# Count blocks that end on a real product instead of a product with zeros, and half-size loop turns where two chunks are left

## What is computed

```
def _sage_layer(h, edge_src, edge_dst, deg_inv, W_self, W_neigh, b):
    msg = h[edge_src]
    agg = jax.ops.segment_sum(msg, edge_dst, num_segments=h.shape[0])
    mean = agg * deg_inv[:, None]
    return h @ W_self + mean @ W_neigh + b
...
deg = jax.ops.segment_sum(jnp.ones_like(edge_dst, dtype=x.dtype), edge_dst, num_segments=N)
deg_inv = 1.0 / jnp.maximum(deg, 1.0)
h = jax.nn.relu(_sage_layer(x, edge_src, edge_dst, deg_inv, W_self0, W_neigh0, b0))
out = _sage_layer(h, edge_src, edge_dst, deg_inv, W_self1, W_neigh1, b1)
...
x = x + _L0_gnn_ref(_layernorm(x, axis=-1), src, dst, ...)
x = x + _L0_ffn_ref(_layernorm(x, axis=-1)[None], L0_ffn_W_fc, L0_ffn_W_proj)[0]
```

## Time and profile before

| | |
|---|---|
| median of the runs | 1630.81 us |
| profiled execution | 1631.58 us |
| its span in the trace | 1629.6 us |
| TensorE busy with products | 1603.5 us |
| stretch with count turns | 60 to 303 us |
| granted TensorE clock, mean | 0.996 |

### The profile page before, as it was taken

How to read it: one execution, slowest core, us unless ns; L and a number is a source line. 1 busy time by engine, 2 the same in 40 slices (tenths; PEclk the granted TensorE clock), 3 DMA queues, 4 the chain that set the end, 5 groups by cost and what they waited for, 6 DMA issues and landing times.

```text
span 1629.6 us, 22403 instructions
## 1 busy us (share of the span) xinstructions
PE 1603.5 (98%) x7709; PEld 1344.4 (83%) x7709; DVE 894.4 (55%) x1613; ACT 462.8 (28%) x816; POOL 97.9 (6%) x190
## 2 busy tenths in 40 slices
PE   7999999999999999999999999999999999999997
PEld 5777667788888888889899899898998888888884
DVE  7786777565212222656334343343443788888868
ACT  3344454211112000114123131130321333333358
POOL 0230134200000000001000000000001000000000
PEclk9999999999999999999999999999999999999998
DMA  7322333467533454558122021120223233333321
GB/s 296 133 104 82 115 114 130 178 246 261 186 103 121 186 206 159 180 194 287 50 78 78 26 103 51 51 103 26 77 69 111 104 116 116 116 116 116 116 91 49
DMA packets 55926, 205.43 MB, mean 126 GB/s; under 512 B 5330, under 2 KB 13852, under 8 KB 50340
## 3 DMA queue, kind: packets, MB, share of 16 engines
q1 hardware_dynamic: 53524, 191.76, 33.3%
q0 software_dynamic: 2320, 12.58, 2.0%
HBM read 153.85 MB, written 50.47 MB: 125 GB/s over the span
## 4 chain that ended last, share of the span: by engine, by line
PE 95%; issue 1%; DVE 1%; DMA 1%; ACT 1%; DVEq 0%; POOL 0%; SPq 0%; ACTq 0%; POOLq 0%
PE bank L1588 26%; PE bank L1569 26%; PE bank L1425 26%; PE bank L1518 11%; PE bank L1374 3%; PE bank L1401 2%; ACT spikes L900 1%; PE bank L1620 0%; DMA w_landing<-w_self 0%; DVE w L1079 0%; DMA pr_raw<-w_proj 0%; DMA at_dram<-counts_tile 0%; DMA rows<-x 0%; DVE key_hot L1026 0%; DVE xt L1067 0%
## 5 line engine op out<-in xcount | busy, mean ns | idle before, releaser
L1425 PE MATMUL bank<-w,xt 128*128 128x512 f32 x1920 | 462.7, 396 | 2.6 <-DVE w L1079 2.6
L1569 PE MATMUL bank<-x2t,fc_w 128*128 128x384 f32 (+1 forms) x2304 | 438.4, 350 | 0.4 <-ACT relu L865 0.4
L1569 PEld LDWEIGHTS bank<-x2t,fc_w 128*128 128x128 f32 x2304 | 411.7, 188 | 25.6 <-issue 0.7
L1425 PEld LDWEIGHTS bank<-w,xt 128*128 128x128 f32 x1920 | 356.8, 189 | 76.9 <-issue 3.3
L1588 PE MATMUL bank<-pr_w,hid 128*128 128x512 f32 (+1 forms) x1824 | 418.7, 390 | 0.0
L1588 PEld LDWEIGHTS bank<-pr_w,hid 128*128 128x128 f32 (+1 forms) x1824 | 338.2, 185 | 75.5
L1291 DVE TENSOR_TENSOR y<-y,bank 128x512 f32<-128x512 f32 (+1 forms) x152 | 104.2, 687 | 214.8 <-PE bank L1588 214.8
L1518 PE MATMUL bank<-z,at 128*128 128x512 f32 x800 | 186.9, 392 | 0.0
L1518 PEld LDWEIGHTS bank<-z,at 128*128 128x128 f32 x800 | 148.8, 188 | 30.2
L860 ACT ACTIVATE pr_w<-pr_raw 128x1024 fp32r<-128x1024 f32 x64 | 67.1, 1049 | 365.6 <-PE bank L1588 362.6
L1234 DVE TENSOR_TENSOR square<-relu 128x384 f32<-128x384 f32 (+1 forms) x96 | 56.9, 592 | 144.2 <-ACT relu L865 144.2
(11 more groups left out here) (127 smaller groups left out, 931.8 us busy)
## 6 DMA issues: line engine op xcount, KB each, us to landing
fc_raw<-w_fc SPq DMA_DIRECT2D x64, 512.0 KB, 4.3
pr_raw<-w_proj SPq DMA_DIRECT2D x64, 512.0 KB, 3.5
xt<-xt_dram SPq DMA_DIRECT2D x24, 1024.0 KB, 5.0
xt_dram<-xt SPq DMA_DIRECT2D x18, 1024.0 KB, 4.3
at<-at_dram SPq DMA_DIRECT2D x20, 640.0 KB, 5.9
part_dram<-rows SPq DMA_DIRECT2D x20, 512.0 KB, 3.8
rows<-part_dram SPq DMA_DIRECT2D x20, 512.0 KB, 4.5
rows<-x SPq DMA_DIRECT2D x18, 512.0 KB, 4.9
```

Source lines behind the costliest of these rows:

```text
L1425: ins = nc.tensor.matmul(bank[:, 2 * (u % 2) + q, :], xt[j][:, a, k, :], w[:, k, b, q * HALF:(q + 1) * HALF], start=(k == 0 and m == 0), s ...
L1569: ins = nc.tensor.matmul(bank[:, 4 + (c if g == 0 else j % 2), 0:n], fc_w[:, j % 2, k, a, :], x2t[g][:, k, v, c0:c0 + n], start=(k == 0 an ...
```

## The change

It has four parts. A window without extra turns now multiplies two of its head chunks, runs its loop, and ends on the third head chunk, which carries `stop` and counts up `hot_used[HEAD_SET]`. A window with extra turns runs the loop to its true end first, in turn 0, and then the turns that run once; the last of them carries `stop`. The product with `zero_w` is gone, and so are `zero_w` and `counts_summed`: ScalarE waits for `hot_used` of the set that ends the block. In 17 windows (`SHORT_TURNS`) the loop of turn 0 covers two chunks a turn instead of four, one in set 1 and one in set 2. And the turns are spread anew: unit 0 of S0 gets 2 turns for 3, unit 4 gets 6 for 7, units 6 and 7 get 7 for 6. There are still 74 turns. On TensorE and VectorE the registers are read and added up after the head, no longer before it.

```diff
+SHORT_TURNS = {0, 6, 9, 10, 11, 12, 13, 18, 27, 31} | set(range(33, 40))
+
+def chunks_of_set(i, j):
+    return 1 if j == 0 and window_of(i) in SHORT_TURNS else LOOP_SET
...
-        [(A0 + 3, 1, 30, 12)] + [(A0 + n, 3, 14, 36) for n in range(4, TILES - 1)] + [(A0 + 9, 1, 12, 12), (S0, 3, 30, 18)]
-        + [(S0 + p, 6 if p in (6, 7) else 7, 0, 48) for p in range(1, 9)]):
+        [(A0 + 3, 1, 30, 12)] + [(A0 + n, 3, 14, 36) for n in range(4, TILES - 1)] + [(A0 + 9, 1, 12, 12), (S0, 2, 40, 10)]
+        + [(S0 + p, 6 if p == 4 else 7, 0, 48) for p in range(1, 9)]):
...
             first, end = registers[2 * (i % 2):2 * (i % 2) + 2]
-            if j > 0:
-                engine.reg_add(first, first, LOOP_CHUNKS)
-            if j < extra_turns(i):
-                engine.reg_add(stop, first, 1)
-                end = stop
-            latest = CHUNKS + HEAD_CHUNKS - 1 + LOOP_CHUNKS * j
+            latest = CHUNKS + HEAD_CHUNKS - 1
+            if j == 0:
+                latest += LOOP_CHUNKS * extra_turns(i)
+                engine.reg_add(edge, first, LOOP_CHUNKS * extra_turns(i))
+                first = edge
+            else:
+                latest += LOOP_CHUNKS * (j - 1)
+                if j > 1:
+                    engine.reg_add(first, first, LOOP_CHUNKS)
+                engine.reg_add(edge, first, 1)
+                end = edge
...
-                with act.Fori(first, end, LOOP_CHUNKS) as g:
+                with act.Fori(first, end, count * len(LOOP_SETS)) as g:
...
-                act.wait_ge(counts_summed, i + 1)
+                if extra_turns(i) > 0:
+                    act.wait_ge(hot_used[ACT_SET], visit)
+                else:
+                    act.wait_ge(hot_used[HEAD_SET], i + 2)
...
             def key_one_hots(i, j):
                 v = window_of(i)
-                first, end = turns_of_step(dve, registers, stop, i, j)
                 if j == 0:
                     dve.wait_ge(current_ready, i + 1)
...
                     ins.then_inc(key_hot_ready[HEAD_SET], 1)
-                with dve.Fori(first, end, LOOP_CHUNKS) as g:
+                count = chunks_of_set(i, j)
+                first, end = turns_of_step(dve, registers, edge, i, j)
+                with dve.Fori(first, end, count * len(LOOP_SETS)) as g:
...
             def step_of_edges(i, j):
-                first, end = turns_of_step(pe, registers, stop, i, j)
+                last = extra_turns(i)
                 if j == 0:
                     if i >= 2:
                         pe.wait_ge(counts_copied, i - 1)
-                    products_of_set(i, HEAD_SET, i + 1, start=True)
-                with pe.Fori(first, end, LOOP_CHUNKS) as g:
-                    for s in LOOP_SETS:
-                        products_of_set(i, s, visit)
-                    pe.reg_add(visit, visit, 1)
-                    pe.reg_add(next_visit, next_visit, 1)
-                if j == extra_turns(i):
-                    nc.tensor.matmul(bank[:, 4 + i % 2, 0:2], zero_w[:, :], iota[0:P, 0:2], start=False,
-                                     stop=True).then_inc(counts_summed, 1)
+                    pe.wait_ge(src_hot_ready, i + 1)
+                    pe.wait_ge(key_hot_ready[HEAD_SET], i + 1)
+                    kept = 0 if last else 1
+                    for c in range(HEAD_CHUNKS - kept):
+                        ins = product_of_chunk(i, HEAD_SET, c, start=(c == 0))
+                    if not kept:
+                        ins.then_inc(hot_used[HEAD_SET], 1)
+                count = chunks_of_set(i, j)
+                first, end = turns_of_step(pe, registers, edge, i, j)
+                with pe.Fori(first, end, count * len(LOOP_SETS)):
+                    turn_of_edges(i, count, stop=(j == last > 0))
+                if last == 0:
+                    product_of_chunk(i, HEAD_SET, HEAD_CHUNKS - 1, stop=True).then_inc(hot_used[HEAD_SET], 1)
```

More of the change, by code:

```diff
@@ L178, in gnn_ffn @@
         at_raw = [tile[:, :, :].bitcast(F32) for tile in at]
-        counts_tile, edge_col, iota, zero_w, current, src_hot, key_hot, dist = put_from(
+        counts_tile, edge_col, iota, current, src_hot, key_hot, dist = put_from(
             at_at, ("counts_tile", [128, COUNT_TILES, TILES, T], F32),
-            ("edge_col", [P, 2, CHUNKS + PAD_CHUNKS], F32), ("iota", [128, WINDOW_COLS], F16), ("zero_w", [P, T], F16),
+            ("edge_col", [P, 2, CHUNKS + PAD_CHUNKS], F32), ("iota", [128, WINDOW_COLS], F16),
             ("current", [P, 2, HEAD_CHUNKS], F32), ("src_hot", [P, 3, max(HEAD_CHUNKS, LOOP_SET), 128], BF16),
@@ L391, in load_ranges, with turns_of_step @@
             return values[0:2], values[2:4]
-        def turns_of_step(engine, registers, stop, i, j):
+        def turns_of_step(engine, registers, edge, i, j):
             if i % 2 == 0 and j == 0:
@@ L737, in _ @@
             registers = range_registers(act, "act")
-            stop = act.alloc_register("act_stop")
+            edge = act.alloc_register("act_edge")
             def src_one_hots(i, j):
-                first, end = turns_of_step(act, registers, stop, i, j)
-                with act.Fori(first, end, LOOP_CHUNKS) as g:
+                count = chunks_of_set(i, j)
+                first, end = turns_of_step(act, registers, edge, i, j)
+                with act.Fori(first, end, count * len(LOOP_SETS)) as g:
                     act.wait_ge(act_hot_ready, visit)
-                    for c in range(LOOP_SET):
-                        chunk = g + (LOOP_SET * LOOP_SETS.index(ACT_SET) + c)
+                    for c in range(count):
+                        chunk = g + (count * LOOP_SETS.index(ACT_SET) + c)
                         ins = nc.scalar.activation(dist[:, c, :], iota[0:P, 0:128], ACT.Square,
@@ L751, in src_one_hots @@
                     act.wait_ge(hot_used[ACT_SET], visit)
-                    nc.scalar.activation(src_hot[:, ACT_SET, 0:LOOP_SET, :], dist[:, :, :], ACT.Relu, bias=1.0,
+                    nc.scalar.activation(src_hot[:, ACT_SET, 0:count, :], dist[:, 0:count, :], ACT.Relu, bias=1.0,
                                          scale=-1.0).then_inc(act_hot_ready, 1)
@@ L1017, in key_one_hots @@
                     ins.then_inc(key_hot_ready[HEAD_SET], 1)
-                with dve.Fori(first, end, LOOP_CHUNKS) as g:
+                count = chunks_of_set(i, j)
+                first, end = turns_of_step(dve, registers, edge, i, j)
+                with dve.Fori(first, end, count * len(LOOP_SETS)) as g:
                     for place, s in enumerate(LOOP_SETS):
                         dve.wait_ge(hot_used[s], visit)
-                        for c in range(LOOP_SET):
-                            chunk = g + (LOOP_SET * place + c)
+                        for c in range(count):
+                            chunk = g + (count * place + c)
                             if s != ACT_SET:
@@ L1364, in _, with product_of_chunk, turn_of_edges @@
             registers = range_registers(pe, "pe")
[L1365 to L1376 removed]
+            edge = pe.alloc_register("pe_edge")
+            def product_of_chunk(i, s, c, start=False, stop=False):
+                return nc.tensor.matmul(bank[:, 4 + i % 2, 0:WINDOW_COLS], src_hot[:, s, c, :], key_hot[:, s, c, :],
+                                        start=start, stop=stop)
+            def turn_of_edges(i, count, stop=False):
+                for s in LOOP_SETS:
+                    if s == ACT_SET:
+                        pe.wait_ge(act_hot_ready, next_visit)
+                    pe.wait_ge(key_hot_ready[s], visit)
+                    for c in range(count):
+                        ins = product_of_chunk(i, s, c, stop=(stop and s == ACT_SET and c == count - 1))
+                    ins.then_inc(hot_used[s], 1)
+                pe.reg_add(visit, visit, 1)
+                pe.reg_add(next_visit, next_visit, 1)
             def step_of_edges(i, j):
[L1379 removed]
+                last = extra_turns(i)
                 if j == 0:
```

47 lines of the change are left out of this document (8 added, 39 removed).

## The result

The changed kernel takes 1636.63 us (median of 7 executions, 1635.22 to 1638.11), the kernel before 1630.81 us (7 executions, 1630.16 to 1632.55). The ratio is 1.0035, with a 95% interval of 1.0025 to 1.0045. So it is slower by some 0.35%, and the forecast of 1634.8 us was 1.8 us too low. The profiled execution of the changed kernel took 1638.0 us, 1.4 us above its median; before it was 0.8 us above. The spans differ by 6.6 us.

The account below looks back on a forecast made before the run. TensorE was taken as the bound before window 14, GpSimd's round through the single head buffer from there on. Terms -7.1 + 9.0 + 2.1 - 0.5 - 0.3 + 1.1 - 0.7 + 0.4 = +4.0 gave 1634.8 us, range 1627.5 to 1639.5.

Parts of the forecast that it names:

- The gain, -7.1 us: Before window 14, TensorE saves 30 chunk products (4.0 us) and 26 closing products (3.1 us).
- The rounds, +9.0 us: Windows 14 to 17 and 19 to 26: release 0.54 us later per round, plus 3.1 us of register stalls; 45.6 us for 12 rounds.
- the first rival: Late release costs no more than the gain: head buffer binds but register work hides; 1630.2 us, no change; 25%.
- the second, that GpSimd's round doesn't decide: TensorE is 98% busy and the gain is simply 9.4 us: 1621.4 us, faster; 17%.
- Window 18: Window between the two groups of rounds: 9 products, 14 dense ones and a register read take 4.8 us, -0.5.
- the end: Behind the last head, 2 products and a closing one go: -0.3 us.
- The stalls in A0: Four even windows stall some 0.25 us at the register read; +1.1 us with the odd ones, bounds 0 and 2.2.
- SyncE's stores follow it: nothing: ScalarE waits for another semaphore at the same time as before, and SyncE's stores follow it; no cost.
- -4.6 forecast: Changed kernel's lead by window 14's head: 4.6 us, from -7.1 + 2.1 + 1.1 - 0.7.
- upper bound: All stalls at their upper bounds: rounds +11.3, A0 +2.2, units +1.0, some +8.5 us in sum, 1639.3 us.
- both terms of the units: VectorE's `take_self` at unit starts: -0.7 us with short turns in S0, +0.4 on a round in the last two units.
- The clock case: TensorE's clock falls to 1.2 GHz for the last rounds' 46 us; time would pass 1645 us; 3%.

Follow-up runs that it names:

- experiment two: Kernel before with only the short loops: in 17 windows the last turn takes two chunks instead of four; 1626.89 us, ratio 0.9972.
- experiment three: Kernel before with only the late release: in windows of one turn the closing product frees the head buffer; 1637.21 us, ratio 1.0038.
- Experiment four: Changed kernel with TensorE's register read and register operation put back ahead of the head products, VectorE's left behind its head; 1634.31 us, ratio 1.0018.
- Experiment seven: Kernel before with only the slots of the changed kernel; 1637.72 us, ratio 1.0038.
- ten: Version six with the turns at the slots of the kernel before; 1624.2 us, ratio 0.9961.
- eleven: Version six at its own slots, with SyncE's store of a tile that ends in a unit's first turn issued first; 1623.29 us, ratio 0.9955.
- eight: Changed kernel with all three head products first and a closing product with zeros in windows of one turn; late reads and slots kept; 1635.96 us, ratio 1.0025.
- six: Changed kernel's blocks, but one-turn windows multiply all head products first and close on zeros; reads ahead of the head; 6 turns in unit 6; 1632.0 us, ratio 1.0006.
- nine: Changed kernel with SyncE's store of a tile that ends in a unit's first turn issued ahead of the load and other store; 1635.43 us, ratio 1.0030.
- one: Changed kernel with the turns at the slots of the kernel before; 1635.69 us, ratio 1.0027.
- five: Changed kernel with two head buffers, used in turn by even and odd windows; 1629.74 us, ratio 0.9988.

## Why the prediction came out right in sign and 1.8 us low

**The gain, -7.1 us: right.** A turn in A0 takes 3.71 us, and 3.42 with a short loop (timeline of TensorE):

```profile
68.88 1.12 PE L1384 MATMUL bank<-key_hot,src_hot 125*128 125x320 bf16 x7
...
72.59 1.29 PE L1384 MATMUL bank<-key_hot,src_hot 125*128 125x320 bf16 x7
...
87.20 0.85 PE L1384 MATMUL bank<-key_hot,src_hot 125*128 125x320 bf16 x5
...
90.62 1.05 PE L1384 MATMUL bank<-key_hot,src_hot 125*128 125x320 bf16 x5
```

Against the earlier trace rows the closing product is worth 3.83 - 3.71 = 0.12 us, as taken, and five times the floor of about 25 ns that the prediction cites from the Trainium skill, page "TensorE: Matmul & The Clock Gate", section "Back-to-back issue gap". The short loops alone gave 3.9 us in experiment two, where the sum had 4.0, and beside it the wait at the start of S0 grew from 1.98 us to 2.5, with half clock behind it.

**The rounds, +9.0 us: right, measured +8.4.** The late release alone gives +6.5 (experiment three). The moved read gives the rest: an even round takes 3.96 us in the mean (forecast 3.98) and an odd one 3.55 (forecast 3.62). Experiment four, with the reads early, makes them 3.55, but for the one that waits for the late store. So the first rival, that the release costs no more than the gain, fell on the stalls, and the second, that GpSimd's round doesn't decide, on the heads that all wait for GpSimd.

**Smaller terms.** Window 18 takes 274.65 to 279.44, 4.8 us as forecast; the end gives 0.4 for 0.3. The stalls in A0 sum to 1.6 us for 1.1, half of it at one head (101.30).

**The step that failed: "SyncE's stores follow it: nothing".** It was argued from when ScalarE copies, not from what stands on SyncE's queue when the store is issued. The new slots move the end of window 7 across the border of a unit, and its store falls behind 1.5 MB. That cost TensorE 2.2 us of waiting and 1.4 us of half clock, with what lies around 4.1 in the profiled execution. Experiment seven shows it in the kernel before, without any other part of the change, and ten and eleven show it from the other side: moving the slots back, or the store ahead, gives 8 to 9 us where nothing hides it, the half clock behind the gaps included. In the changed kernel the rounds of 3.55 us and more hide the second late store (window 15's). So the two costs overlap:

| median, us | slots of before | new slots |
|---|---|---|
| blocks of before | 1630.8 | 1637.7 |
| changed blocks | 1635.7 | 1636.6 |

Each alone costs 5 to 7 us, both together 6.

**A wait that wasn't seen.** The forecast had no term for S0's first turn, where before stands for 1.98 us for VectorE. Slot 40 in place of 30 takes 1.5 us of that out of unit 0 (its dense products take 13.45 us with four chunk products fewer, instead of 15.52). Of the four parts of the change this is the good one, and the row that named the wait stood there: 2.2 us for `key_hot`.

**The account to window 14's head:** -4.6 forecast, -1.5 at the start of S0, -0.5 ahead of the first turn, where the change has no part, +0.5 in A0, +4.1 for the late store, some +0.8 at unit starts (where the shorter turns gave nothing back on the whole) make -1.2; the trace has -0.8. The remaining 0.4 us aren't placed. So it is in part luck that the forecast came within 1.8 us: the store and the unit starts went against two terms that it didn't have either. Between the profiled executions, against which its sum is made, the spans differ by 6.6 us where it had 4.0.

**A slip in the upper bound.** Its terms sum to +8.0 us, or to +8.7 if the 1.0 stands for both terms of the units, where the prediction says some +8.5. No chance changes by it.

**The clock case** had 3 in 100, for the whole last stretch. There it stayed at 1.00 in spite of the gaps at each head. It fell in one other place, for 3 us.

**What stays open.** The mean granted clock of every execution is on record, and in three experiments the time goes with it. In eight, two executions with 0.996 and 0.997 took 1632.1 and 1632.3 us, and six with 0.993 to 0.995 took 1634.6 to 1638.0. In six, four with 0.996 and 0.997 took 1629.2 to 1631.7, and seven with less took 1631.4 to 1634.8. In two, three with 0.997 took 1625.3 to 1625.8, and two with 0.995 took 1628.0 and 1628.2, while the three with 0.996 lie on both sides (1625.9, 1627.9 and 1627.9); the median of 1626.89 lies between the groups, so the 3.9 us are a mixture of both. So the clock falls in some executions and not in others, and it makes part of these spreads. At full clock eight lies some 4.4 us below the changed kernel's median, near the 5 to 7 expected. In the changed kernel and in nine the time doesn't go with the clock: at 0.997 nine took 1633.6 to 1637.2. Why nine's profiled execution lies 4.1 us under the changed one's, but its median only 1.2, isn't shown.

## What to carry to other kernels

Where a producer with one buffer is the bound, the time of the release decides, not the amount of work: here a semaphore raised 0.54 us later in 12 rounds cost 6.5 us, nearly all of the 7.1 that the removed products give. When work moves to other slots, follow the stores and loads as well: see for each transfer what now stands ahead of it on its queue, and whose next write waits for its landing. And a cost can lie hidden under another, so undo them together (here two head buffers, early reads and an early store) before judging any of them.

## What the runs showed of the hardware

- A store of 640 KB landed 2.9 us after its issue when nothing was ahead of it, and 7.5 us when it was issued right behind a load of 1 MB and a store of 512 KB on the same queue.
- One gap on TensorE of 2 to 2.7 us can bring the granted clock down to 0.5 for some 3 us behind it, at a price of 1.2 to 1.6 us: it did after 1.95 us in experiment ten, 2.1 in seven, 2.2 in the changed kernel, 2.3 in six, 2.5 in two, 2.6 in eight and 2.65 in one, and it did not after 1.98 in the kernel before, 2.3 in four and 2.3 in seven. After 3.5 us in six and 3.9 in five it stayed there for some 7 us. The gaps of 0.8 to 1.1 us at each head never did this.
- A register read on TensorE cost nothing that shows when the sequencer came to it ahead of the head's semaphore (experiment four: 3.55 us for odd and even rounds alike). Behind two products of a head that it was held for, it made a round longer by 0.1 to 0.9 us, where the read itself takes 0.33.
